# When SP asks for four of the ten early tiles of the last stage

## What is computed

```
x   = x + tanh(g_xattn) * latent_cross_attention(layernorm(x), ctx_512, ...)   # x: 16 x 112 x 512
xn2 = layernorm(x)
logits = xn2 @ gate_w.T ; top 8 of 64 experts, weights by softmax
out = sum over the 8 experts of weight * down(silu(gate(xn2)) * up(xn2))
    + sigmoid(xn2 @ sh_gate1.T) * sh_down(silu(xn2 @ sh_gate.T) * (xn2 @ sh_up.T))
x   = x + tanh(g_ffn) * out
```

## Time and profile before

| what | us |
|---|---|
| median of 3 runs | 1497.38 |
| lowest and highest of them | 1494.94, 1502.37 |
| the profiled execution | 1504.56 |
| its span, first to last instruction | 1502.7 |
| mean granted TensorE clock over the span | 0.981 of full |

### The profile page before, as it was taken

The page is one execution under the profiler, slowest core; times in us unless marked ns, Lnnn a source line. Parts: engine busy times, 40 slices in busy tenths (PEclk is TensorE's granted clock), DMA queues, the critical chain, the costliest instruction groups (busy, mean ns, idle before and its releaser), DMA issues.

```text
span 1502.7 us, 25078 instructions
## 1 busy us (share of the span) xinstructions
PE 1411.7 (94%) x7680; PEld 1156.9 (77%) x7680; DVE 1147.9 (76%) x2603; ACT 670.9 (45%) x1558; POOL 783.4 (52%) x858
## 2 busy tenths in 40 slices
PE   7999999999999999999999999985499999999976
PEld 6767887877788787788787778763489998998743
DVE  6768883499886289989449988453488999998588
ACT  3332772011576011277201147230377778777521
POOL 4655772145675468877347887334235434333322
PEclk9999999999999999999999999997699999999999
DMA  8899896465797778730467861496899999999698
GB/s 265 297 324 313 276 297 203 129 196 186 225 297 222 250 227 256 226 97 11 139 217 231 255 225 42 139 351 206 277 330 314 338 359 360 364 334 338 209 427 366
DMA packets 164504, 380.11 MB, mean 253 GB/s; under 512 B 20088, under 2 KB 55570, under 8 KB 162578
## 3 DMA queue, kind: packets, MB, share of 16 engines
q1 hardware_dynamic: 110726, 245.49, 49.2%
q10 hardware_dynamic: 33036, 70.72, 14.3%
q0 software_dynamic: 20608, 62.28, 11.9%
HBM read 238.82 MB, written 139.59 MB: 252 GB/s over the span
## 4 chain that ended last, share of the span: by engine, by line
PE 69%; DVE 10%; DMA 8%; POOL 6%; issue 5%; ACT 2%; SPq 0%; ACTq 0%; POOLq 0%; DVEq 0%
PE bank L858 18%; PE bank L860 17%; PE bank L859 17%; PE bank L965 7%; DMA p_in<-parts 4%; PE bank L994 4%; DMA parts<-y_sb,to_row 3%; PE bank L1164 3%; POOL slot_rows L2039 2%; POOL q_rope L2022 2%; DVE q_sin L1322 1%; POOL prob L2028 1%; DVE row_max L1336 1%; PE bank L950 1%; PE bank L940 1%
## 5 line engine op out<-in xcount | busy, mean ns | idle before, releaser
L2022 POOL TENSOR_TENSOR q_rope<-q_rope,q_sin 128x448 f32<-128x448 f32 x192 | 215.3, 1151 | 121.0 <-DVE q_sin L1322 120.3
L2098 POOL DMA_INDIRECT parts<-y_sb,to_row x140 | 138.0, 986 | 216.1 <-ACT y_sb L1923 166.5
L2028 POOL TENSOR_TENSOR prob<-prob,row_inv 128x375 f32<-128x375 f32 x218 | 175.8, 813 | 80.1 <-DVE row_inv L1344 73.9
L2039 POOL DMA_INDIRECT slot_rows<-rows,pos_i x112 | 110.7, 988 | 105.8 <-DVE count L1430 76.2
L1322 DVE TENSOR_TENSOR q_sin<-bank,sin_q 128x448 f32<-128x448 f32 (+1 forms) x256 | 158.2, 618 | 4.0
L965 PE MATMUL bank<-q_rope,m_w 128*128 128x448 f32 x384 | 156.8, 542 | 2.2 <-POOL q_rope L2022 1.0
L1336 DVE TENSOR_REDUCE row_max<-bank 128x1 f32<-128x375 f32 x224 | 118.8, 535 | 36.2 <-PE bank L860 35.5
L1776 ACT ACTIVATE prob<-bank,row_max 128x375 f32<-128x375 f32 x224 | 128.3, 573 | 5.4 <-DVE row_max L1336 5.4
L1923 ACT ACTIVATE y_sb<-bank,own 96x512 f32<-96x512 f32 (+4 forms) x140 | 90.6, 686 | 72.2 <-PE bank L860 56.6
L1318 DVE TENSOR_TENSOR q_rope<-bank,cos_q 128x448 f32<-128x448 f32 x192 | 118.1, 615 | 0.2 <-POOL q_rope L2022 0.2
L994 PE MATMUL bank<-ident,prob 128*125 128x128 f32 x672 | 112.5, 276 | 3.0 <-DVE prob_t0l L1357 2.5
(11 more groups left out here) (374 smaller groups left out, 4386.6 us busy)
## 6 DMA issues: line engine op xcount, KB each, us to landing
w_ex<-in_w_ex SPq DMA_DIRECT2D x64, 768.0 KB
slot_rows<-blank SPq DMA_DIRECT2D x64, 612.0 KB
p_in<-parts SPq DMA_DIRECT2D x13, 2048.0 KB, 16.8
m_w<-m_dram SPq DMA_DIRECT2D x48, 192.0 KB, 3.5
x_g<-slot_rows ACTq DMA_DIRECT2D x16, 476.0 KB
x_g<-slot_rows ACTq DMA_DIRECT2D x12, 510.0 KB
wq_s0h<-wq_dram ACTq DMA_DIRECT2D x23, 256.0 KB
wq_s0l<-wq_dram ACTq DMA_DIRECT2D x23, 256.0 KB
```

The source lines that it names most:

```text
L2022: pool.tensor_tensor(o[:, c, :], o[:, c, :], q_sin[:, c, :], ALU.add).then_inc(s_radd, 1)
L2028: pool.tensor_tensor(prob[i][:], prob[i][:], row_inv[:, i:i + 1].to_broadcast([P, L]), ALU.mult)\
L2039: pool.indirect_dma_start(slot_rows, bass.IndirectOffsetOnAxis(ap=pos_i[i][:, k:k + 1], axis=0), rows[i][:], None).then_inc(s_slots[i], 16)
L2098: pool.indirect_dma_start(parts, bass.IndirectOffsetOnAxis(ap=to_row[x % NROW][0:size, t:t + 1], axis=0), y_sb[x % NY][t][0:size, :], None)\
```

## The change

`TILES_AHEAD = 6` takes the place of `EARLY_TILES = 10` in the two loops of SP that ask for tiles. At the pass's begin SP asks for tiles 0 to 5; tiles 6 to 9 are asked for behind the last context, ahead of tiles 10 to 12. The guards and the buffers stay as they are.

```diff
 EARLY_TILES = 10
+TILES_AHEAD = 6
 EARLY_BATCHES = -(-EARLY_TILES * P // S)
...
                 sp.dma_start(spare[:], a["c_spare"]).then_inc(s_spare, 16)
-                for i in range(EARLY_TILES):
+                for i in range(TILES_AHEAD):
                     load_base(i)
...
             sp.wait_ge(s_ctx, NBK * B)
             wait_stored(LAST - 1)
-            for i in range(EARLY_TILES, LAST_TILE):
+            for i in range(TILES_AHEAD, LAST_TILE):
                 load_base(i)
```

## The result

**Time.** The changed kernel took 1504.60 us in the median of 17 runs (1495.56 to 1509.87), the kernel before 1497.38 in 17 runs taken beside them (1493.18 to 1502.93). The ratio is 1.0033, 95% interval [1.0018, 1.0048]: slower by 7.2 us in the medians. The profiled execution took 1506.44 us, span 1504.6. One thing has to be known to read these and all later numbers: executions of one and the same kernel on one chip spread over up to 16 us, here mostly in a lower and an upper group some 7 us apart, so I also count executions above 1503 us, a bound set after seeing them. Here they are 13 of 17 with the change and none of 17 without. The profiled execution of before, 1504.56, stands above all 17.

A forecast was written before the change was run, and what follows sets the result against it. The prediction took the routing of the last two batches, not bytes, to set the attention's end. Its terms, 0 + 0 + 0 with ends of -2.2 and +6.0, on the runs' 1497.4 gave 1497 us, range 1488 to 1505.

The forecast's parts named there:

- the forecast case: Removed loads, added loads and passed queues each cost 0 around the attention's end, so no change; chance 0.70.
- Removed, gain 0: At the pass's begin, eight fewer SP issues and 2.1 MB less relieve nothing awaited: gain 0, at most 2.2 us.
- Added, cost 0: Behind the last context, eight more issues and 2.1 MB fit in idle SP and DMA time: cost 0, at most 6.0.
- the full 6.0: Worst delay in us of batch 15's stores by the moved tiles' transfer, against SP's 5.7 us wait for the order.
- Queues passed, cost 0: Moved loads pass stores and weights on SP and run beside POOL's scatters, perhaps 1 or 2 us; taken as 0.
- The skill's rule: DMAs of SP and GpSimd share 16 engines, so scatters and tiles share 6.0 us: 1503.4 instead of 1497.4.
- Rival 1: PE's 11.15 us wait before batch 14's router comes from traffic and vanishes, with slow clock 14.3 us: 1483.1 to 1490.3; chance 0.16.
- Rival 2: The wait before batch 14's router grows by 6.0 us transfer, perhaps 4.2 of slow clock: 1503.4 to 1507.6; chance 0.14.
- The deciding point: A wait above 11.15 us between the last context and batch 14's router in the profile after would show growth.
- the sum's starting point: The sum starts from the runs' median of 1497.4 us, not the profiled 1504.6.

The follow-up runs named there:

- e9: The change itself run again on chip 6 against the kernel before (1492.34 us): 1491.08 us, ratio 0.9999 [0.9986, 1.0011].
- e2: Removal alone on chip 15 (tiles 6 to 9 never loaded, tiles 0 to 3 read instead) against the kernel before: 1490.44 us, ratio 0.9985.
- e7: Removal alone on chip 6 (tiles 6 to 9 never loaded) against the kernel before: 1491.79 us, ratio 0.9998.
- e14: Removal alone on chip 5 (tiles 6 to 9 never loaded) against the kernel before: 1502.93 us, ratio 1.0013 [0.9993, 1.0032].
- e3: Addition alone on chip 15 (ten early tiles, 6 to 9 loaded again behind the last context) against the kernel before: 1491.30 us, ratio 1.0002.
- e4: Changed kernel with TILES_AHEAD = 0 on chip 15, all ten tiles behind the last context, against the kernel before: 1499.21 us, ratio 1.0050.
- e6: Changed kernel with TILES_AHEAD = 3 on chip 13, seven tiles moved, against the kernel before: 1504.45 us, ratio 1.0024 [1.0003, 1.0046].
- e15: Changed kernel on chip 5 with batch 13's first scatter held until batch 14's routing has begun, against the kernel before: 1497.95 us, ratio 0.9980.
- e5: The change again, only a blank line more, on chip 13 against the kernel before (1498.81 us): 1504.37 us, ratio 1.0031.
- e18: The change as it was, on chip 14 against the kernel before (1497.28 us): 1497.77 us, ratio 1.0000 [0.9975, 1.0025].
- e13: The change as it was, on chip 5 against the kernel before (1500.06 us): 1505.29 us, ratio 1.0025 [1.0004, 1.0046].

## Why the prediction was right and wrong

*The number.* 1504.6 lies in the range (1488 to 1505) and the ratio of 1.0033 within 0.5%, but the forecast of 1497.0 is 7.6 below, and the interval excludes no change. So the forecast case, all costs 0, did not come on this chip. It did come, as worked out, on a chip without late counts (e9, 0.9999).

*Removed, gain 0.* Right as a sum on chips 15 and 6: e2 and e7 are 0.9985 and 0.9998. "No loss, since only work is taken out" is not shown wrong, but not shown right either where counts come late (1.0013 in e14).

*Added, cost 0.* Right on chips 15 and 6, with the cover mis-sized. I gave "12.6 remain" of SP's idle; 8.4 remained, since the loads too came late, and began at 1031.81 and not at 1025. I gave the stores' landing "the full 6.0" at worst against 5.7 of slack: e3 shows 5.4 more (8.6 for 3.2) against 5.5 of the order's wait. That term was right almost to the edge, and e4 shows what is behind it, 6.7 us from the last scatter to the first gathered tile.

*Queues passed, cost 0.* Right. POOL's scatters stay at 0.94 us, and PE waits for no DMA at the last heads.

*The skill's rule.* By the Trainium skill's page "DMA: Bandwidth & Descriptors", section "Issuing engines are not separate DMA queues", scatters and tiles share the engines and the prediction made 1503.4 of it. The time came out near that, but not by that rule: e9 has scatters and tiles on full engines (1.03, 373 GB/s) at no cost, and seven tiles moved (e6) took no longer than four, as far as the intervals tell.

*Rival 1, the wait is made by traffic and goes.* Wrong: 11.6 us, the traffic before it lower (0.87 against 0.98), and e15, on a chip with late counts, has full traffic (1.00) with a wait of 2.0.

*Rival 2, the wait grows: slower.* The side was right, its mechanism not. The deciding point, a wait above 11.15 us, was passed with 11.6, by 0.45; that is worth 0.45 and not 7. The moved bytes came after the wait.

*The step that failed* is the sum's starting point, "against the runs 1497.4", with the wait before batch 14's router put at nothing in it. The three zeros themselves, nothing for the removed loads, the added ones and the queues passed, hold where no count comes late. I took the wait from one profiled execution as a fixed piece that either stays, goes or grows, and put the difference of 7.2 us between profile and median down as an offset, which only rival 1 read, half: "the ordinary runs may hold only half of that". What the profiles show in its place is a wait that is there in some executions and not in others, 9.5 to 11.9 us in seven of nine without the pause on the chips with late counts, 1.6 at most in the other two. The counts say that what moved is how often it is long. On chip 5 the share above 1503 went from 7 of 29 to 10 of 12, and the executions of before above the bound lie at 1505.0 in the mean, the others at 1498.5: (0.83 - 0.24) x 6.5 = 3.8 us, where the means differ by 4.3 (1504.4 and 1500.1). That is an estimate, since the bound cuts a spread without a gap. No row of one profile can give that share; the runs' own spread could have warned, as the profile stood above the highest of the three runs shown.

*What is shown and what stays open.* Shown: without late counts the change costs nothing that can be measured (e9 on chip 6; on chip 15 only its parts were run); on the three sets of runs where it was slower most of its executions are in the upper group, and all profiled executions above 1503 us hold the long wait, while e5's, at 1498.2, doesn't (e18's, at 1500.92, does); a pause in POOL's row of scatters takes that wait and the upper group away with the change in place (chip 5: 10 of 12 to none; over chips 5 and 14 none of 36 with the pause against 11 of 58 of before). Argued, not shown: that the time of the unprofiled executions is made by the same wait. Open: by what way a row of scatters holds PE's counts; why two of the chips never show it, with the same unbroken row; and why the change makes it likelier in three sets of runs and not on chip 14. The removal alone has 11 of 24 above 1503 us against 15 of 52 of before (above 1502 us 15 of 24 against 18 of 52), and the long wait in both its profiles there; the addition alone 5 of 12 against 8 of 23, and none in its one profile. That points to the removal, and so does that the late counts begin before the moved loads (the DMA share from 1000 to 1010 was 1.06 before and 0.64 after), but no interval names the part: it is argued, not shown.

No version beat both kernels everywhere. The changed kernel with the pause was faster than before on chip 5 (0.998) and not told from it on chip 14; it wasn't run on a chip without late counts, where its pause should, by its expectation, cost 3 to 6 us of POOL's row.

## What to carry to other kernels

When the profiled execution stands 7 us above the median, look first at the longest wait that is put down to "issue" or "remote": it may be in the profile and not in most runs, so its length is no fixed term of a sum, and a change is then to be judged by how often it is long, on more than one chip. Count the semaphore updates that the trace holds, too: where some are missing, "issue" and "remote" may only mean that the count wasn't recorded. A transfer moved in front of a store on the same queue is free up to the slack of what waits for the store's landing, and that slack has to be added up over all waits in a row (3.2 and 6.4 here). Where an engine issues a long unbroken row of scatters beside a critical exchange between engines, try a break in it before moving bytes about.

## What the hardware showed that I had not expected

- Counts of PE reach ACT, DVE and SP up to 11.3 us after the last matmul's end (e6; 11.2 in the kernel before, 10.9 in e13), in a stretch in which PE, DVE and ACT then all stand: in e13 0.96, 0.69 and 0.60 us busy of 10. The lag is 1.2 us at most elsewhere in the spans of before and after, up to the last microseconds.
- Of nine profiles without the pause on chips with late counts, the seven with sixteen scatters 0.30 to 0.36 us apart hold the long wait and the two with a break of 1.75 and 3.24 us don't. The eight of the two other chips have the unbroken row and no lag above 0.1 us.
- The traces of the two chips without late counts hold 6066 to 6069 updates of semaphores by the engines, those of all the others 5468 to 5536, for the same program but for a few lines.
- With a pause of 3.57 us in sixteen scatters the largest lag was 2.4 us where it was 10.9, with fuller DMA engines (1.00 against 0.70).
- Chips differ: the same kernel before has a median of 1491.15 and 1492.34 on two chips without late counts, and 1497.28 to 1500.40 in the five other sets of runs.
- An issue on SP's queue took up to 2.89 us, against some 0.5 for most, when twenty-six loads of 256 KB were asked for in a row (e4).
